# Building the gather table of a deformable convolution: four projected copies in PSUM, or one copy stored four times

## Chip, core and metric

The kernel runs on one NeuronCore of a Trainium2 chip. The metric is the device time of one execution in microseconds (us); of the kernel before, three executions were timed, and one more was profiled.

## The reference

Eight images of 56 x 56 pixels with 128 channels pass through four layers. Layer 1 is a selective-scan layer (called VSS here, a state-space scan in four directions). Layers 0, 2 and 3 are deformable convolutions, and the change is in these:

```python
xp = x @ w_in + b_in                                     # project every pixel
h = gelu(depthwise 3x3 conv of x, batch norm)
offset = (h @ w_off + b_off).reshape(N, H, W, 4, 9, 2)   # 4 groups, 9 points
mask = softmax((h @ w_msk + b_msk).reshape(N, H, W, 4, 9))
pad = jnp.pad(xp, 1)                                     # 58 x 58 padded pixels
# for each pixel, group and point: four corners, weighted bilinearly
samp = v(y0, x0)*w00 + v(y0, x0+1)*w01 + v(y0+1, x0)*w10 + v(y0+1, x0+1)*w11
y = einsum(samp, mask) @ w_out + b_out
x = x + gamma1 * layer_norm(y)
x = x + gamma2 * layer_norm(gelu(x @ w_fc1 + b_fc1) @ w_fc2 + b_fc2)
```

A group has 32 of the 128 channels. A corner's value is thus 32 floats, 128 bytes.

## The kernel before

**Stages.** One deformable layer on one image is a stage; there are 24, numbered 0 to 23 in the order of `stage_order`: (0,0), (0,1), ... with (layer, image) pairs of layers 0, 2 and 3 mixed. The scans of layer 1 run beside the stages, on the same engines.

**The table.** Each stage gathers from a table in DRAM (`table0` or `table1`, by the stage's parity). Row 4f + g of it belongs to padded pixel f and group g, and holds the four corners' 32 channels side by side, 512 bytes, so that one gathered row brings all four corners. The table of stage k+1 is made while stage k gathers.

**Making it.** A table step is `("at", k, i, 0)` on TensorE and `("at", k, i, 1)` on ScalarE and SyncE, i = 0 to 25, one for 128 padded pixels. TensorE projects the same pixels four times, shifted by 0, 1, 58 and 59 pixels (L1080), each with a one-row matmul that adds the bias and masks the border (L1081), into the four quarters of PSUM bank `d_pr1`. ScalarE copies the bank to `d_pst` (L834), with the channels put in the table's order, and SyncE stores 128 x 2048 bytes with one DMA (L573). `d_pst` is a single buffer: the copy of a step waits for the landing of the step before (semaphores `tab0` and `tab1`).

**Other ahead work.** The same bank `d_pr1` serves in turn the transposed input chunks (`ax`, L1068, loaded by `axl`, L548), the depthwise convolution (`ac`, L1092, stored by L580) and the offsets and masks of four pixel tiles (`pr`, L1104 on TensorE, then VectorE up to the indices `d_idx`, L1439). SyncE issues all these DMAs on one hardware queue, in the order of the program.

**Gathering.** GpSimd issues 882 indirect DMAs a stage (L674), 12 for each of the stage's 74 weigh steps, into one of five `d_g` buffers. VectorE weighs a buffer (L1247), TensorE adds it up (L943), and frees it. GpSimd starts a group of tiles only when its `d_idx` is there. The output chain of a pair of tiles (`ch`) follows.

**Order.** A planner (`Planner`) writes one list of items that every engine walks through in order. It puts scan steps and ahead steps between weigh steps. A scan step of a quiet kind takes a whole tick; the work behind a scan (`g`, `m`, `p`: gate, output projection, MLP, and the next image's projection) takes half ticks, and is thus packed twice as densely. I call that stretch the after-scan stretch: it lies in stages 3, 6, 8, 11, 13, 16, 18 and at the end of stage 20. `("ax", k, c)` for a layer-2 stage needs chunk c of the scan's output, which is stored by L651 and read back by L548 after a wait for the store's landing. Where a stage's work ahead is not done when its predecessor ends, the planner drains it there, while GpSimd has nothing to gather.

## Time and profile before

| | us |
|---|---|
| median of 3 runs (32655.79 to 32672.39) | 32657.38 |
| profiled execution, its own time | 32686.79 |
| span of the profiled execution | 32684.8 |
| GpSimd busy | 24416.8 (75%) |
| TensorE matmul busy | 24822.2 (76%) |
| VectorE busy | 22462.3 (69%) |
| ScalarE busy | 12136.3 (37%) |
| mean granted TensorE clock | 0.833 |

The span is the time from the first to the last instruction of the one core. Busy shares are of that span. The granted clock is 1 at 2.4 GHz and 0.5 at 1.2 GHz. GpSimd's time between two gathers is not counted as busy: the profile calls it issue.

### The profile page before, as it was taken

To read this page: it belongs to the slowest core of one execution; us is meant where nothing else is said; L and a number is where in the kernel's file an instruction comes from. 1 tells how busy PE (TensorE), PEld (TensorE's weight loads), DVE (VectorE), ACT (ScalarE), POOL (GpSimd) and SP (SyncE) were. 2 spreads that over 40 slices of the span, in tenths; PEclk is the share of its full clock that TensorE was granted. 3 is DMA by queue.
4 is the path that set the end of the run, shared out by engine and by line. 5 is a ranking of instruction groups with operands and counts; after the bars stand their busy time and mean duration, and the time that the engine had idled before them with its cause. 6 is when DMAs were issued, how large, how long until landed. Compare 5 with 4: busy or idle time off the path is not lost.

```text
span 32684.8 us, 293367 instructions
## 1 busy us (share of the span) xinstructions
PE 24822.2 (76%) x101616; PEld 16206.4 (50%) x101616; DVE 22462.3 (69%) x31704; ACT 12136.3 (37%) x20755; POOL 24416.8 (75%) x21172
## 2 busy tenths in 40 slices
PE   7587788877878788787877888778787887774544
PEld 5454455544545455455444555445444554454443
DVE  1278877888588868885888678876888688841211
ACT  1144434443444434443444444434444444420100
POOL 5777777777677777776777777777777777757767
PEclk6688888888888888888888888888888888886666
DMA  2211122111211121122111211112111221122211
GB/s 64 66 55 52 54 61 58 57 52 54 69 48 58 52 64 55 50 58 67 50 54 51 67 54 56 54 55 65 49 56 52 64 58 49 53 59 60 63 54 52
DMA packets 1191499, 1854.81 MB, mean 57 GB/s; under 512 B 388074, under 2 KB 747036, under 8 KB 1190012
## 3 DMA queue, kind: packets, MB, share of 16 engines
q0 software_dynamic: 677376, 1388.62, 15.2%
q1 hardware_dynamic: 512636, 447.43, 4.3%
q8 instruction: 803, 13.16, 0.2%
q14 instruction: 684, 5.60, 0.1%
HBM read 1569.35 MB, written 265.21 MB: 56 GB/s over the span
## 4 chain that ended last, share of the span: by engine, by line
POOL 64%; issue 18%; PE 13%; DVE 4%; ACT 1%; DMA 1%; SPq 0%; DVEq 0%; POOLq 0%; ACTq 0%
POOL d_g L674 64%; PE d_p L943 3%; DVE l_wk L1212 1%; PE d_pr L1081 1%; PE d_pr L1080 1%; PE d_pr L1092 1%; PE l_acc L929 1%; PE l_pm L978 1%; PE l_pc L1056 1%; DVE l_wk L1234 1%; DVE d_g L1247 1%; PE d_pr L1146 0%; DVE l_wk L1202 0%; PE l_pm L1031 0%; PE l_pm L1017 0%
## 5 line engine op out<-in xcount | busy, mean ns | idle before, releaser
L674 POOL DMA_INDIRECT d_g<-table,d_idx x21168 | 24416.6, 1153 | 8226.0 <-issue 6426.2
L943 PE MATMUL d_p<-d_g,c_ident 128*128 128x128 f32 x43200 | 6992.9, 335 | 3787.9 <-DVE d_g L1247 3786.3
L943 PEld LDWEIGHTS d_p<-d_g,c_ident 128*128 128x128 f32 x43200 | 6720.0, 247 | 4581.6 <-DVE d_g L1247 3658.1
L929 PE MATMUL l_acc<-l_wk,c_ident 128*128 128x448 f32 x14336 | 7141.1, 627 | 0.0
L1212 DVE TENSOR_TENSOR_SCAN l_wk<-l_wk,l_carry 128x448 f32<-128x448 f32 x6144 | 6715.0, 1133 | 0.0
L1247 DVE TENSOR_TENSOR d_g<-d_g,d_wt 128x1536 f32<-128x1536 f32 x1776 | 3103.7, 1748 | 5238.2 <-DMA d_g<-table,d_idx 5235.1
L1202 DVE TENSOR_TENSOR l_wk<-l_wk,l_pb 128x896 f32<-128x896 f32 x3584 | 3865.1, 1078 | 1585.0 <-PE l_pb L899 1577.0
L707 ACT ACTIVATE l_carry<-l_wk 128x2 f32<-128x2 f32 x3584 | 735.1, 205 | 10325.8 <-DVE l_wk L1212 10322.2
L717 ACT ACTIVATE l_wk<-l_wk,l_a 128x448 f32<-128x448 f32 x7168 | 4362.6, 656 | 14.2 <-DVE l_wk L1276 0.4
L929 PEld LDWEIGHTS l_acc<-l_wk,c_ident 128*128 128x128 f32 x14336 | 3100.6, 217 | 1820.9 <-issue 1699.3
L899 PE MATMUL l_pc<-l_spl,c_sel 96*128 96x448 bf16 x3584 | 1398.0, 390 | 3354.8 <-DVE l_wk L1234 3345.2
L1234 DVE TENSOR_TENSOR l_wk<-l_wk,l_pc 128x896 f32<-128x896 f32 x3584 | 3797.9, 1060 | 3.1 <-PE l_pc L899 2.4
L899 PEld LDWEIGHTS l_pc<-l_spl,c_sel 96*128 96x128 bf16 x3584 | 359.3, 100 | 4414.6 <-DVE l_wk L1234 4363.6
L899 PE MATMUL l_pb<-l_spl,c_sel 96*128 96x448 bf16 x3584 | 1355.9, 378 | 166.8 <-DVE l_wk L1202 158.5
L717 ACT ACT_TABLE_LOAD x1147 | 1471.6, 1283 | 20.0
L1081 PE MATMUL d_pr<-c_mix 1*128 1x128 f32 (+1 forms) x4992 | 1355.2, 355 | 0.0
L1080 PE MATMUL d_pr<-d_win,d_xt 128*128 128x128 f32 (+1 forms) x4992 | 1312.5, 349 | 37.0 <-ACT d_pst L834 23.3
L1092 PE MATMUL d_pr<-d_xt,d_diag 128*128 128x448 f32 x3024 | 1261.9, 557 | 7.6 <-ACT d_xt L825 5.2
L1080 PEld LDWEIGHTS d_pr<-d_win,d_xt 128*128 128x128 f32 (+1 forms) x4992 | 867.8, 211 | 496.1 <-issue 238.3
L1485 DVE BATCH_NORM_STATS2 d_bs<-d_pr 128x6 f32<-128x128 f32 (+1 forms) x1200 | 295.2, 285 | 1132.8 <-PE d_pr L1148 784.1
L1212 DVE TENSOR_TENSOR_SCAN l_wk<-l_wk 128x448 f32<-128x448 f32 x1024 | 1057.2, 1072 | 0.0
L1081 PEld LDWEIGHTS d_pr<-c_mix 1*128 1x128 f32 (+1 forms) x4992 | 824.8, 206 | 352.5 <-issue 106.6
(173 smaller groups left out, 22413.6 us busy)
## 6 DMA issues: line engine op xcount, KB each, us to landing
d_g<-table,d_idx POOLq DMA_INDIRECT x21168, 2.6
table<-d_pst SPq DMA_DIRECT2D x600, 256.0 KB
hd<-d_hst SPq DMA_DIRECT2D x168, 224.0 KB
d_htc<-hd SPq DMA_DIRECT2D x144, 256.0 KB
d_xin<-mid SPq DMA_DIRECT2D x112, 224.0 KB, 3.0
mid<-d_xo SPq DMA_DIRECT2D x192, 128.0 KB
d_xres<-mid SPq DMA_DIRECT2D x192, 128.0 KB
d_xin<-in_x SPq DMA_DIRECT2D x56, 224.0 KB, 3.1
```

The source lines that it names most:

```text
L674: e.indirect_dma_start(out=m.g[Q % SLOTS][:, j, :], out_offset=None, in_=m.table[k % 2], in_offset=bass.IndirectOffsetOnAxis(ap=m.idx[G % ...
L717: ins = e.activation(m.dA[(NSTEP * i + q) % 3][:, h, :], m.dt[P % 2][:, h, :], ACT.Exp, scale=m.aa[:, kd, h, n:n + 1])
L899: return e.matmul(bank[:, 0:448], m.sel[:, row + n:row + n + 1].to_broadcast([96, 128]), m.spl[P % 2][:, :], start=True, stop=True)
L929: ins = e.matmul(m.acc[:, h, 0:448], m.ident[:, :], m.hb[x % 4][:, h, :], start=(n == 0), stop=(n == 15))
L943: ins = e.matmul(m.p0[:, t % 2 * 128:t % 2 * 128 + 32 * w], m.ident[:, :], m.g[Q % SLOTS][:, w * p:w * p + w, 32 * r:32 * r + 32], start=( ...
L1080: e.matmul(m.r[1][0:n, cr * 128:cr * 128 + 128], m.xf[:, pos:pos + n], m.win[:, :], start=True, stop=False)
L1081: ins = e.matmul(m.r[1][0:n, cr * 128:cr * 128 + 128], m.mask[0:1, mo:mo + n], m.rowa, start=False, stop=True)
L1092: ins = e.matmul(m.r[1][:, 0:448], m.diag[:, j, :], m.xt[:, 8 * c + dy:8 * c + dy + 8, dx:dx + 56], start=(j == 0), stop=(j == 8))
L1202: e.tensor_tensor(m.hb[x % 4][:, :, :], m.dtu[P % 2][:, :, :], bc(m.pb[:, 0:448], 1, 2), ALU.mult).then_inc(s["f_pb"], 1)
L1212: ins = e.tensor_tensor_scan(m.hb[S % 4][:, h, way], m.dA[S % 3][:, h, way], m.hb[S % 4][:, h, way], ini, ALU.mult, ALU.add)
L1234: e.tensor_tensor(m.hb[x % 4][:, :, :], m.hb[x % 4][:, :, :], bc(m.pc[:, 0:448], 1, 2), ALU.mult).then_inc(s["f_pc"], 1)
L1247: e.tensor_tensor(g, g, wt, ALU.mult).then_inc(s["weighed"], 1)
```

## The change

Each padded pixel is projected once. The 3364 padded pixels are 27 tiles of 128; a table step now takes four tiles (`QUADS`, seven steps, the last with three tiles), one tile to each quarter of the bank. ScalarE copies the bank as it is. SyncE then stores each tile once for each corner: source row p, 128 floats, goes to the four group rows of padded pixel 128i + p - shift, at the corner's 128 bytes of each. That is 106 DMAs a stage with runs of 128 bytes, in place of 26 with runs of 2048 bytes. Most have 128 source rows; near the table's ends some have 127, 70, 69, 105, 106, 35 or 36.

```diff
+QUADS = [list(range(q, min(q + 4, 27))) for q in range(0, 27, 4)]
...
-        tables = deque((i, min(6, max(0, (128 * i + 127 + 59) // PW - 1) // 8)) for i in range(26))
+        tables = deque((j, min(6, max(0, (128 * x[-1] + 127) // PW - 1) // 8)) for j, x in enumerate(QUADS))
...
-        self.pst = sb("d_pst", [128, 4, 4, 32])
+        self.pst = sb("d_pst", [128, 4, 128])
...
+def corner(i, cr):
+
+    f0 = 128 * i - PW * (cr // 2) - cr % 2
+    p = max(0, -f0)
+    return f0 + p, p, min(128 * i + 128, PW * PW, NTAB + 128 * i - f0) - 128 * i - p
...   SyncE
-            e.dma_start(m.table[k % 2][f0 * 4:(f0 + n) * 4, :].rearrange("(p g) c -> p (g c)", g=4),
-                        m.pst[0:n].rearrange("p g r c -> p (g r c)")).then_inc(s[f"tab{T % 2}"], 16)
+            table = m.table[k % 2].rearrange("(f g) (r c) -> f g r c", g=4, c=32)
+            for x, i in enumerate(QUADS[j]):
+                for cr in range(4):
+                    first, p, n = corner(i, cr)
+                    if n > 0:
+                        e.dma_start(table[first:first + n, :, cr, :], m.pst[p:p + n, x, :].rearrange("p (g c) -> p g c", g=4),
+                                    ).then_inc(s[f"tab{T % 2}"], 16)
...   GpSimd, ahead of a stage's first gather
-        for b, v_ in enumerate(both(26 * k + 25)):
-            e.wait_ge(s[f"tab{b}"], v_)
+        for T in (7 * k + 5, 7 * k + 6):
+            e.wait_ge(s[f"tab{T % 2}"], J.tables(T))
...   ScalarE
-                e.wait_ge(s[f"tab{(T - 1) % 2}"], 16 * ((T - 1) // 2 + 1))
-            e.activation(m.pst[0:n], m.r[1][0:n, :].rearrange("p (r g c) -> p g r c", r=4, g=4),
-                         ACT.Copy).then_inc(s["f_r1"], 1)
+                e.wait_ge(s[f"tab{(T - 1) % 2}"], J.tables(T - 1))
+            whole = 4 if j < 6 else 2
+            ins = e.activation(m.pst[:, 0:whole, :], m.r[1][:, 0:128 * whole].rearrange("p (t c) -> p t c", c=128), ACT.Copy)
+            if j == 6:
+                ins = e.activation(m.pst[0:36, 2, :], m.r[1][0:36, 256:384], ACT.Copy)
+            ins.then_inc(s["f_r1"], 1)
...   TensorE
-            for cr in range(4):
-                pos = f0 + PW * (cr // 2) + cr % 2
+            for x, i in enumerate(QUADS[j]):
+                pos = 128 * i
+                n = min(128, PW * PW - pos)
...
-                e.matmul(m.r[1][0:n, cr * 128:cr * 128 + 128], m.xf[:, pos:pos + n], m.win[:, :], start=True, stop=False)
+                e.matmul(m.r[1][0:n, x * 128:x * 128 + 128], m.xf[:, pos:pos + n], m.win[:, :], start=True, stop=False)
```

The planner has 19 table steps fewer to place in each stage, so its list changes around them. Two places matter to the prediction. The first is SyncE's order of DMAs in stage 6, while it prepares stage 7, a layer-2 stage, beside the after-scan work: `mid<-l_xb` stores a chunk of the scan's output, `d_xin<-mid` reads it back for the table's stage, `l_wk<-xn`, `l_xb<-mid` and `l_wk<-mid` are loads of the after-scan work. Before:

```order
L573 DMA table<-d_pst 128x512
L651 DMA mid<-l_xb 112x4x128
L548 DMA d_xin<-mid 112x4x128
L643 DMA l_wk<-xn 128x448
L646 DMA l_xb<-mid 112x4x128
L626 DMA l_wk<-mid 112x4x128
L611 DMA d_xres<-in_x 128x2x128
L573 DMA table<-d_pst 128x512 x2
L633 DMA xn<-l_wk 128x448
```

The same place in the changed kernel:

```order
L589 DMA table<-d_pst 512x1x32
L589 DMA table<-d_pst 508x1x32
L589 DMA table<-d_pst 280x1x32
L589 DMA table<-d_pst 276x1x32
L589 DMA table<-d_pst 512x1x32 x12
L667 DMA mid<-l_xb 112x4x128
L561 DMA d_xin<-mid 112x4x128
L659 DMA l_wk<-xn 128x448
L662 DMA l_xb<-mid 112x4x128
L642 DMA l_wk<-mid 112x4x128
```

One DMA ahead of the chunk's store has become sixteen, with 512 runs each; the later single stores between the loads are gone.

The second place is TensorE at the end of stage 22, whose successor, stage 23, works on the same image. The first row adds up stage 22's last but one weigh step, the 128x64 rows with x12 its last one, and L1133 and L1139 are the output chain. Before, with the table steps shortened to their first pair:

```order
L943 MATMUL d_p<-d_g,c_ident 128x64 x24
L1080 MATMUL d_pr<-d_win,d_xt 128x128
L1081 MATMUL d_pr<-c_mix 128x128
...
L1133 MATMUL d_pr<-c_ident,d_x 128x128 x2
L1080 MATMUL d_pr<-d_win,d_xt 128x128
L1081 MATMUL d_pr<-c_mix 128x128
...
L943 MATMUL d_p<-d_g,c_ident 128x64 x12
L1139 MATMUL d_pr<-d_yt,d_fc 128x256 x4
```

The same place in the changed kernel:

```order
L961 MATMUL d_p<-d_g,c_ident 128x64 x24
L1150 MATMUL d_pr<-c_ident,d_x 128x128 x2
L961 MATMUL d_p<-d_g,c_ident 128x64 x12
L1156 MATMUL d_pr<-d_yt,d_fc 128x256 x4
L1163 MATMUL d_pr<-d_fc,d_ht 128x128 x4
```

Two table steps of eight matmul groups each stood ahead of the stage's last weigh step, and none does now.

## Rows read from the trace of the kernel before

**Rows 1.** The page: busy time of each engine, and the chain that ended last
```profile
PE 24822.2 (76%) x101616; PEld 16206.4 (50%) x101616; DVE 22462.3 (69%) x31704; ACT 12136.3 (37%) x20755; POOL 24416.8 (75%) x21172
...
POOL 64%; issue 18%; PE 13%; DVE 4%; ACT 1%; DMA 1%; SPq 0%; DVEq 0%; POOLq 0%; ACTq 0%
```

**Rows 2.** Waits of GpSimd: cause, us in total, times, longest
```profile
POOL d_g L674 <- issue: 6426.2, 21086, 0.3
POOL d_g L674 <- DVE d_idx L1439: 1384.2, 22, 270.0
POOL d_g L674 <- PE d_p L943: 415.2, 59, 30.5
```

**Rows 3.** Gathers alone, stages 21 and 12: window, length, busy (count), clock, DMA
```profile
29600.00:30235.00 635.00, 477.21 (x482) 0.66 0.20 56
17300.00:17860.00 560.00, 444.40 (x370) 0.85 0.18 52
```

**Rows 4.** Waits of GpSimd for TensorE within stages 3, 8, 13
```profile
POOL d_g L674 <- PE d_p L943: 28.1, 7, 12.2
POOL d_g L674 <- PE d_p L943: 47.1, 5, 22.7
POOL d_g L674 <- PE d_p L943: 34.0, 5, 14.8
```

**Rows 5.** Waits of GpSimd for indices after stages 1, 20, 22
```profile
POOL d_g L674 <- DVE d_idx L1439: 45.1, 1, 45.1
POOL d_g L674 <- DVE d_idx L1439: 221.5, 1, 221.5
POOL d_g L674 <- DVE d_idx L1439: 121.7, 1, 121.7
```

**Rows 6.** Timeline at the start: start, us, instruction, idle before
```profile
31.93 0.60 ACT L834 ACTIVATE d_pst<-d_pr 128x512 f32<-128x512 f32 x1 [5.95 <-PE d_pr L1081]
32.59 0.80 PE L1080 MATMUL d_pr<-d_win,d_xt 128*128 128x128 f32 x2 [0.69 <-ACT d_pst L834]
38.48 0.60 ACT L834 ACTIVATE d_pst<-d_pr 128x512 f32<-128x512 f32 x1 [5.95 <-PE d_pr L1081]
```

**Rows 7.** L1080, then L1081, up to 270 us: PE and PEld busy, clock, DMA
```profile
0.00:270.00 270.00, 76.39 (x208) 47.66 (x208) 0.69 0.16 51
0.00:270.00 270.00, 76.65 (x208) 47.75 (x208) 0.69 0.16 51
```

**Rows 8.** DMA queues in 40.2 to 43.3 us, around one input load
```profile
DMA packets 557, 0.39 MB, mean 125 GB/s; under 512 B 32, under 2 KB 480, under 8 KB 557
...
q1 hardware_dynamic: 557, 0.39, 38.8%
```

**Rows 9.** SyncE's table stores (ns of one issue), and landing of L548
```profile
L573 SPq DMA_DIRECT2D table<-d_pst x624: 319/320/975, 26.0 to 31492.0; - x156
...
DMA to landing us min/median/max: 2.6/3.1/6.9
```

**Rows 10.** Timeline between stages 22 and 23
```profile
31389.66 0.74 PE L1080 MATMUL d_pr<-d_win,d_xt 128*128 128x128 f32 x2
...
31401.94 5.38 PE L943 MATMUL d_p<-d_g,c_ident 128*128 128x64 f32 x24
...
31461.49 0.72 ACT L844 ACTIVATE d_hst<-d_pr,d_bnv 128x448 f32<-128x448 f32 x1 [7.12 <-PE d_pr L1092]
...
31492.41 0.33 SPq L603 DMA_DIRECT2D d_htc<-hd  x1
```

**Rows 11.** After-scan stretch of stage 6: all engines, then L1080 alone
```profile
8219.00:8620.00 401.00, 346.84 (x1602) 245.35 (x1602) 144.19 (x414) 150.73 (x213) 272.87 (x262) 0.86 0.29 83
8219.00:8620.00 401.00, 32.07 (x128) 21.24 (x128) 0.86 0.29 83
```

**Rows 12.** Idle before L1068 in all, and before L1292 in 8219 to 8640 us
```profile
DMA d_xin<-mid: 148.5, 34
...
DVE l_st L1292 <- DMA l_wk<-mid: 34.6, 5, 8.7
```

More of the change, by code:

```diff
@@ L485, in __init__, with tables @@
         self.total = total
+    def tables(self, T):
+        return sum(16 for x in range(T % 2, T + 1, 2) for i in QUADS[x % 7] for cr in range(4) if corner(i, cr)[2] > 0)
     def full(self, *key):
@@ L565, in sync_program @@
         elif kind == "at" and item[3] == 1:
-            _, k, i, _ = item
-            T = 26 * k + i
-            f0 = 128 * i
-            n = min(128, NTAB - f0)
-            if k >= 2 and i == 0:
-                e.wait_ge(s["weighed"], NQ * (k - 1))
-            e.wait_ge(s["f_r1"], J.free("t", k, i))
-            e.dma_start(m.table[k % 2][f0 * 4:(f0 + n) * 4, :].rearrange("(p g) c -> p (g c)", g=4),
-                        m.pst[0:n].rearrange("p g r c -> p (g r c)")).then_inc(s[f"tab{T % 2}"], 16)
+            _, k, j, _ = item
+            T = 7 * k + j
+            if k >= 2 and j == 0:
+                e.wait_ge(s["weighed"], NQ * (k - 1))
+            e.wait_ge(s["f_r1"], J.free("t", k, j))
+            table = m.table[k % 2].rearrange("(f g) (r c) -> f g r c", g=4, c=32)
[5 more added lines that the diff above has]
+                                    ).then_inc(s[f"tab{T % 2}"], 16)
         elif kind == "ac" and item[3] == 3:
@@ L827, in scalar_program @@
         elif kind == "at" and item[3] == 1:
-            _, k, i, _ = item
-            T = 26 * k + i
-            n = min(128, NTAB - 128 * i)
-            e.wait_ge(s["p_r1"], J.full("t", k, i))
+            _, k, j, _ = item
+            T = 7 * k + j
+            e.wait_ge(s["p_r1"], J.full("t", k, j))
             if T:
-                e.wait_ge(s[f"tab{(T - 1) % 2}"], 16 * ((T - 1) // 2 + 1))
-            e.activation(m.pst[0:n], m.r[1][0:n, :].rearrange("p (r g c) -> p g r c", r=4, g=4),
-                         ACT.Copy).then_inc(s["f_r1"], 1)
+                e.wait_ge(s[f"tab{(T - 1) % 2}"], J.tables(T - 1))
[4 more added lines that the diff above has]
+            ins.then_inc(s["f_r1"], 1)
         elif kind == "ac" and item[3] == 3:
@@ L1070, in tensor_program @@
         elif kind == "at" and item[3] == 0:
-            _, k, i, _ = item
-            f0 = 128 * i
-            n = min(128, NTAB - f0)
-            if i == 0:
+            _, k, j, _ = item
+            if j == 0:
                 e.wait_ge(s["da"], 48 * (k + 1))
-            e.wait_ge(s["f_r1"], J.use["t", k, i])
-            for cr in range(4):
-                pos = f0 + PW * (cr // 2) + cr % 2
+            e.wait_ge(s["f_r1"], J.use["t", k, j])
+            for x, i in enumerate(QUADS[j]):
+                pos = 128 * i
+                n = min(128, PW * PW - pos)
                 mo = pos if pos < PW else pos - 57 * PW + 290 if pos + n > 57 * PW else PW + pos % PW
-                e.matmul(m.r[1][0:n, cr * 128:cr * 128 + 128], m.xf[:, pos:pos + n], m.win[:, :], start=True, stop=False)
-                ins = e.matmul(m.r[1][0:n, cr * 128:cr * 128 + 128], m.mask[0:1, mo:mo + n], m.rowa, start=False,
+                e.matmul(m.r[1][0:n, x * 128:x * 128 + 128], m.xf[:, pos:pos + n], m.win[:, :], start=True, stop=False)
+                ins = e.matmul(m.r[1][0:n, x * 128:x * 128 + 128], m.mask[0:1, mo:mo + n], m.rowa, start=False,
                                stop=True)
```

## The prediction

> **What bounds the kernel now.** I read the page first. GpSimd is busy 75% of the span, and its issue time adds 6426.2 us, so 30,843 of 32,684.8 us are gathers; the chain that ended last says the same with POOL 64% and issue 18% [rows 1, 2]. Next come GpSimd's waits. There are only two kinds: 1384.2 us for indices, in 22 waits, of which 270.0 us is the start of the kernel, and 415.2 us for TensorE to free a `d_g` buffer [rows 2]. The change touches no gather, so all it can win is in these 1800 us, and it can lose by making new ones. TensorE at 76% and ScalarE at 37% are no bound by their shares.
>
> A gather's own time is the next thing to settle, since the change puts more packets in the hardware queue. In stage 21, where no scan runs, a gather takes 477.21 / 482 = 0.99 us; in stage 12, with the scan, 444.40 / 370 = 1.20 us, at a slightly lower DMA share [rows 3]. So it is the scan's work that stretches gathers, and DMA traffic doesn't follow it. I cost the extra traffic at nothing for GpSimd's own time; if it did cost, each 1% would be 244 us.
>
> The waits by place: most boundaries between stages cost 16 to 50 us (after stage 1, 45.1), but the one after stage 20 costs 221.5 and the one after stage 22 121.7 [rows 5]. By the planner's list, table steps still run in these two and at the start, and nowhere else: elsewhere they end 18 or more weigh steps before the stage's end, so those boundaries stay. The waits for TensorE lie in the after-scan stretches: 28.1, 47.1 and 34.0 us in stages 3, 8 and 13, 109 together [rows 4], and of the 415.2 the other 306 nearly all in stages 6, 11 and 16.
>
> **What a table step costs now.** At the start one follows the other every 38.48 - 31.93 = 6.55 us: eight groups of matmuls in 38.48 - 32.59 = 5.9 us, the last one's end included, so 0.725 us each, and 0.7 us for the copy and the turn [rows 6]. In 270 us the 26 steps hold TensorE for 76.39 + 76.65 = 153 us; neighbours overlap (0.80 us long, 0.725 us apart), so it is about 141 us of its time [rows 7]. The granted clock there is 0.69 in the mean, a mix of both levels. In stage 6 it is 0.86, and 128 records, 16 steps, take 32.07 us on L1080 [rows 11]; doubled for L1081, 4 us a step.
>
> **Removed.** Of 104 pairs of matmul groups a stage 27 stay. 26 copies become 7, with one small extra copy.
>
> Start: 141 x 77/104 = 104 us, and 19 turns of 0.7 us = 13 us: 117 us.
>
> Stages 3, 8, 13: the planner had 12 to 15 table steps, two or three depthwise chunks and input chunks at the after-scan stretch. Now it has placed all of that before the 33rd weigh step, ahead of the stretch. That is over 50 us of TensorE less (12 steps of 4 us), more than each wait of 28 to 47 us. I take all 109 us as gone. Gathers that then run beside VectorE's work, in place of waiting beside it, take about (1.20 - 0.99) / 1.20 = 18% longer, so 109 x 0.82 = 90 us are won.
>
> Stages 6, 11, 16: by the end of the stretch some 19 steps of 4 us (76 us) have gone, and 27 pairs (27 us) come in: close to 45 us less a stage, 135 us in all.
>
> After stage 22: two table steps stand ahead of the last weigh step and hold it from 31389.66 to 31401.94 us, 12.3 us, with the output chain behind it [rows 10]. They are gone. After the last depthwise copy at 31461.49 came five steps and then the offset load at 31492.41, 31 us [rows 10]; now two steps come, whose price follows.
>
> **Added: the bursts.** Each step now issues 16 DMAs (the last 10). An issue takes 0.32 us, some 0.37 us apart: 16 take 5.9 us [rows 9]. They hold 8192 runs of 128 bytes, 512 for each of 16 engines. No row of the kernel before shows a DRAM write in such short runs. From below: only the issue counts, 5.9 us a burst. From above: around one input load, 557 packets, most of them 512-byte rows, take 38.8% of 16 engines in 3.1 us, 34.6 ns each [rows 8]; 512 of those are 17.7 us. I take 12 us, in the middle, as a quarter of the bytes should make a packet shorter, not longer. The landing adds 2.6 us [rows 9]. Per stage that is 77 us of queue time spread over 1,350 us.
>
> The Trainium skill (DMA: Bandwidth & Descriptors, Specifications) puts the least transfer for full rate at 512 bytes and says that below it the engine reads, modifies and writes. It speaks against this change; no run here shows it yet, and I make it a rival below. The same page (Why a DMA increments its semaphore by 16 and not by 1) says that a DMA runs on the largest number of engines up to 16 that divides both sides' outer sizes; by it the 127-row store of the first step would use one engine, 508 runs. No row here shows that.
>
> Where do bursts cost? At the start they mostly lie beside 18 us of other TensorE work. The last two steps don't: ScalarE's copy of step 6 waits until the burst of step 5 has landed, 12 + 2.6 us, of which TensorE covers 4.4 us, and then ten issues (3.7 us) and some 3 us of data stand ahead of the offset load. About 17 us; start: 117 - 17 = 100 us won (between 9 and 25 for the tail: 92 to 108).
>
> After stage 22: 5.1 + 14.6 + 0.6 + 3.7 + 3 = 27 us in place of 31, plus the 12: 15 us won. After stage 20 three steps fewer, at 6.55 us or a bit more each, less the same tail: 15 us won.
>
> In stages 6, 11, 16 a burst goes out just before the chunk's store and read-back, and SyncE waits for the store's landing before it issues the read and all loads behind it (the order rows of SyncE). TensorE (L1068) and VectorE (L1292) wait for these loads, both in order, so weigh steps behind them are late. Already now TensorE waits 148.5 us in 34 times there, 4.4 us each, and VectorE up to 8.7 us [rows 12]. I count 11 bursts so placed in the three stages, 12 us each, 132 us; and some 12 more input chunks whose transposes follow their load directly, 4.4 us each, 53 us. With the 135 us off, these stages lose about 50 us, of which TensorE's idle 14% there (346.84 of 401 us busy [rows 11]) takes some: I put a loss of 35 us (from 55 won at 5.9 us a burst to 120 lost at 17.7).
>
> Elsewhere bursts lie 35 us or more apart beside the scan, and five `d_g` buffers of 17.5 us each (12 gathers of 1.20 + 0.30 us) cover a wait of 12 us. Without that cover it would be some 130 bursts at about 10 us each, 1,300 us.
>
> **Sum.** 100 + 15 + 15 + 90 - 35 = 185 us won. Against the profiled execution: span 32,685 - 185 = 32,500 us; its own time, 32,686.8, lies 2 us above the span. The median of runs lies 29 us below that, 32,657.4 - 185 = 32,472, rounded to 32,470 us.
>
> **Rivals.** (a) Gain eaten: bursts at the upper price of 17.7 us and nothing absorbed. Start 92, boundaries 5 each, stages 3, 8, 13 only 60, the three dense stages 120 lost: 40 us won, 32,620 us. For it: SyncE sits in front of every load. Against it: a packet with a quarter of the bytes.
>
> (b) Slower: a short DRAM write costs twice a 512-byte packet, 69 ns, 35 us a burst, from which the dense stages lose 11 x 35 + 53 - 135 = 300 us, the start is paced by bursts of 38 us (7 of them, 20 us lost), the two boundaries lose 15 each, and 90 are won: 260 us slower, 32,920 us. It turns at about 23 us a burst, 44 ns a write. For it: nothing here writes DRAM in runs under 512 bytes. Against it: even in the stretch around the input load [rows 8], with its mean of 700 bytes a packet, the price is only 34.6 ns, and I know no reason in these rows for twice that. The Trainium skill's rule of read-modify-write would be this case.
>
> (c) More won: all waits for TensorE go (415 x 0.82 = 340 us) with cheap bursts, and 110 + 25 + 25 us: 500 us, 32,160 us. Against it: the read-back chain in the dense stages stays.
>
> (d) No effect at all, since GpSimd sets the time: within 65 us, as in (a) with the start's gain lost too. Against it: the start's 117 us are TensorE's alone.
>
> **How the numbers follow.** The forecast, 100 to 330 us won, gets 0.6; (a) and (d) together 0.18; (b) 0.15; (c) 0.07. The forecast's own range is 32,330 to 32,590 us. 8 in 10: from 32,320 to 32,690 us, which leaves out (c), most of (b). A measurement of this kernel tells about 0.2%, 65 us, from no change. Faster by more: 0.6 + 0.07 + a small part of (a) = 0.68. Within it: 0.16. Slower: 0.16.
>
> **What would show it.** The first gather should start near 170 us. Stages 3, 8 and 13 should show no wait for TensorE. In stages 6, 11 and 16 waits of L1086 (the former L1068) and L1309 for DMA should be over 300 us, and GpSimd's waits for TensorE about as before. Landing of input loads, 3.1 us now, should have a tail to 15 us. Gathers should still take 0.99 us in stage 21. The prediction is wrong if a burst takes over 23 us, if gathers take longer beside bursts, or if ScalarE's wait for `tab` holds up the scan.

## The result, and the profile after

The changed kernel takes 32290.69 us (median of 4 runs, 32266.03 to 32311.03) against 32656.58 us of the kernel before (4 runs beside it, 32650.71 to 32672.39): ratio 0.9887, 95% interval 0.987 to 0.9904, 366 us less. I had forecast 185 us less and a range down to 32,320 us: the right direction, half the size, and just outside the range.

The head of the page after the change, the waits of GpSimd in the whole span (us, times, longest), and the chain that ended last:

```profile
span 32297.3 us, 279615 instructions
...
PE 23220.6 (72%) x94224; PEld 14960.8 (46%) x94224; DVE 22461.6 (70%) x31704; ACT 11892.0 (37%) x20322; POOL 24335.8 (75%) x21172
...
q1 hardware_dynamic: 1731788, 447.55, 6.2%
...
POOL 71%; issue 19%; PE 6%; DVE 2%; ACT 1%; DMA 1%; SPq 1%; POOLq 0%; DVEq 0%; ACTq 0%
```
```profile
POOL d_g L690 <- issue: 6434.7, 21115, 0.3
POOL d_g L690 <- DVE d_idx L1456: 1291.3, 24, 197.6
POOL d_g L690 <- PE d_p L961: 193.4, 29, 18.8
```

TensorE gave up 4 points of its share and stays off the bound; in the chain that ended last it has 6% where it had 13%. Of GpSimd's two kinds of wait, that for TensorE more than halved (from 415.2) and that for indices fell by 93 (from 1384.2) [rows 2]; GpSimd's own busy time fell by 81 us as well [rows 1], which nothing in my working foresaw. Two waits between stages (after stages 10 and 15, 30.5 and 25.6 us) are put down to TensorE before and to indices after. Like with like, TensorE's fell from 359 to 193 us and the indices' from 1440 to 1291.

The span is 387.5 us shorter. To place it I took, for each of the 24 stages, the time from its first gather to the end of its last, and the gap to the next stage, out of both traces:

```
place                                before     after   difference
first gather begins                   282.1     166.8     -115.3
stages 3, 8, 13                      3969.3    3873.5      -95.8
stage 18                             1297.1    1281.0      -16.1
stages 6, 11, 16                     4112.8    4059.7      -53.1
gap after stage 20                    221.2     197.3      -23.9
gap after stage 22                    121.4     104.3      -17.1
the other 17 stages                 21822.9   21749.4      -73.5
the other gaps                        820.6     827.6       +7.0
```

(The first line counts from some 11.6 us before the page's zero.) The first wait and the waits after stages 20 and 22, as GpSimd shows them, answer to 270.0 [rows 2] and to [rows 5]:

```profile
POOL d_g L690 <- DVE d_idx L1456: 155.2, 1, 155.2
...
POOL d_g L690 <- DVE d_idx L1456: 197.6, 1, 197.6
...
POOL d_g L690 <- DVE d_idx L1456: 104.6, 1, 104.6
```

Stage by stage, stage 3 shows no wait for TensorE any more, and stages 8 and 13 show what is left of [rows 4]:

```profile
POOL d_g L690 <- PE d_p L961: 2.8, 1, 2.8
...
POOL d_g L690 <- PE d_p L961: 0.3, 1, 0.3
```

**The end of the start.** The timeline from 116 to 147 us shows the tail that the last two table steps leave:

```profile
121.02 0.60 ACT L850 ACTIVATE d_pst<-d_pr 128x512 f32<-128x512 f32 x1 [3.49 <-PE d_pr L1098]
121.64 21.33 SPq L589 DMA_DIRECT2D table<-d_pst  x26
...
134.04 0.38 ACT L850 ACTIVATE d_pst<-d_pr 128x256 f32<-128x256 f32 x1 [12.42 <-DMA table<-d_pst]
...
143.02 0.52 SPq L619 DMA_DIRECT2D d_htc<-hd  x1
```

ScalarE's copy of step 6 waits 12.42 us for the stores of step 5, and then ten more issues stand in SyncE's queue ahead of the offset load. From the copy of step 5 to the offset load it is 143.02 - 121.02 = 22.0 us.

**The burst.** One issue of a table store, and the landing of an input load (DMA from issue to landing, us); then the DMA queue over 11 us in which a burst runs nearly alone (packets, MB, share of 16 engines):

```profile
L589 SPq DMA_DIRECT2D table<-d_pst x2544: 512/639/5614, 25.9 to 31105.5; - x196
```
```profile
DMA to landing us min/median/max: 2.5/3.1/5.8
```
```profile
q1 hardware_dynamic: 7541, 0.94, 55.0%
```

An issue takes 0.64 us and not 0.32 as before [rows 9]: 16 of them 10.2 us. The packets take 0.55 x 16 x 11 / 7541 = 12.8 ns each, so 512 for an engine are 6.6 us. A burst is paced by SyncE's issues and not by its data. No input load took more than 5.8 us to land, so where a load is late it is because SyncE hasn't issued it.

The first burst of each stage is longer, 15.5 to 17.0 us, where the others take 10.9 us at the median. Its third store takes some 5 us to issue, and it stands behind the store with 127 source rows, 508 runs. Here is that third store in stage 0's table, and the hardware queue in 28 to 32 us, while SyncE is held up:

```profile
L589 SPq DMA_DIRECT2D table<-d_pst x1: 5028/5028/5028, 27.3 to 27.3; - x1
```
```profile
q1 hardware_dynamic: 375, 0.05, 9.5%
```

In these 4 us 375 packets start, one every 10.7 ns, where the burst above starts 7541 in 11 us, one every 1.5 ns. In e4, where the same 127 rows are 127 runs, no issue takes over 2.1 us.

**The dense stretch.** After-scan stretch of stage 6, the same 401 us of the stage as in [rows 11]: all engines, then L1097 (the former L1080) alone; then what ended TensorE's idle time before L1086 in it, and GpSimd's waits for TensorE in it (49.3 us in 7 times before the change):

```profile
8061.00:8462.00 401.00, 316.72 (x1461) 219.28 (x1462) 144.75 (x415) 149.71 (x209) 257.10 (x248) 0.86 0.34 86
...
8061.00:8462.00 401.00, 11.09 (x48) 7.63 (x48) 0.86 0.34 86
```
```profile
PE d_pr L1086 <- DMA d_xin<-mid: 42.1, 6, 8.7
```
```profile
POOL d_g L690 <- PE d_p L961: 69.2, 7, 12.2
```

TensorE does 42 us less on the two table lines (2 x 32.07 before, 2 x 11.09 now) and waits 42 us for input chunks. SyncE's timeline shows what stands in front of two of these loads:

```profile
8126.48 15.72 SPq L589 DMA_DIRECT2D table<-d_pst  x16
8142.24 0.63 SPq L667 DMA_DIRECT2D mid<-l_xb  x1
8145.11 0.31 SPq L561 DMA_DIRECT2D d_xin<-mid  x1
...
8236.46 10.87 SPq L589 DMA_DIRECT2D table<-d_pst  x16
8247.38 0.62 SPq L667 DMA_DIRECT2D mid<-l_xb  x1
...
8250.25 0.32 SPq L561 DMA_DIRECT2D d_xin<-mid  x1
```

That is the order I had forecast, burst in front of chunk store in front of read-back, and bursts of about the length that I had forecast (10.9 to 15.7 us). In stage 6 the trade came out at a loss of 5 us. But stages 11 and 16 won 17 and 41 us. Over the whole span the waits for input loads are, by L1086's own row and by TensorE's two queues apart (us, times):

```profile
DMA d_xin<-mid: 349.0, 65
```
```profile
PEld d_pr L1086 <- DMA d_xin<-mid: 178.5, 33, 10.3
PE d_pr L1086 <- DMA d_xin<-mid: 170.4, 32, 10.0
...
DVE l_st L1309 <- DMA l_wk<-mid: 266.5, 45, 18.6
```

The row by line adds up the weight load's wait and the matmul's, which are the same wait. I had read its 148.5 us in 34 times [rows 12] as 34 waits of TensorE; they are 17, of 72.4 us, and they lie in the whole span and not in the three dense stages, where my prediction put them. TensorE waits 98 us more than before. In the three dense stages it is 116.8 us in 18 waits against 20.8 in 4; stage 6 has the 42.1 us above.

### The profile page after: what moved, and what is told of

It is laid out like the page before. It is cut to its first block, busy times and chain, and to the rows that moved or that the text cites. A ratio compares the mean times of both kernels' runs of the same rounds, so it can differ in the third digit from the quotient of the medians.

```text
span 32297.3 us, 279615 instructions
## 1 busy us (share of the span) xinstructions
PE 23220.6 (72%) x94224; PEld 14960.8 (46%) x94224; DVE 22461.6 (70%) x31704; ACT 11892.0 (37%) x20322; POOL 24335.8 (75%) x21172
## 4 chain that ended last, share of the span: by engine, by line
POOL 71%; issue 19%; PE 6%; DVE 2%; ACT 1%; DMA 1%; SPq 1%; POOLq 0%; DVEq 0%; ACTq 0%
POOL d_g L690 71%; PE d_p L961 2%; PE d_pr L1109 1%; SPq L589 1%; DVE l_wk L1229 0%; PE l_pc L1074 0%; PE l_pm L996 0%; DVE d_g L1264 0%; PE d_pr L1163 0%; DMA d_g<-table,d_idx 0%; PE l_acc L947 0%; PE d_pr L1123 0%; DMA mid<-l_xb 0%; PE l_pm L1049 0%; PE l_pm L1035 0%
## 5 line engine op out<-in xcount | busy, mean ns | idle before, releaser
L1219 DVE TENSOR_TENSOR l_wk<-l_wk,l_pb 128x896 f32<-128x896 f32 x3584 | 3866.5, 1079 | 989.3 <-PE l_pb L917 982.7
L1109 PEld LDWEIGHTS d_pr<-d_xt,d_diag 128*128 128x128 f32 x3024 | 588.5, 200 | 586.9 <-issue 559.4
L996 PE MATMUL l_pm<-l_yx,l_diag 128*128 128x448 f32 x2016 | 822.4, 546 | 4.1 <-ACT l_xb L775 4.1
L1156 PE MATMUL d_pr<-d_yt,d_fc 128*128 128x256 f32 (+1 forms) x2496 | 738.0, 424 | 93.2 <-ACT d_ht L902 72.5
L917 PEld LDWEIGHTS l_pb<-l_spl,c_sel 96*128 96x128 bf16 x3584 | 371.2, 104 | 933.2 <-DVE l_wk L1219 589.6
```

The source lines that it names most:

```text
L917: return e.matmul(bank[:, 0:448], m.sel[:, row + n:row + n + 1].to_broadcast([96, 128]), m.spl[P % 2][:, :], start=True, stop=True)
L996: ins = e.matmul(m.pm[:, 0:448], m.cdiag[:, 9 * h + j, :], m.grid[:, h, 8 * c + dy:8 * c + dy + 8, dx:dx + 56], start=(j == 0), stop=(j == 8))
L1109: ins = e.matmul(m.r[1][:, 0:448], m.diag[:, j, :], m.xt[:, 8 * c + dy:8 * c + dy + 8, dx:dx + 56], start=(j == 0), stop=(j == 8))
L1156: ins = e.matmul(bank[:, f * 256:f * 256 + nt * n], m.fc1[:, (2 * f2 + f) * 128:(2 * f2 + f) * 128 + 128], m.x1t[:, 0:nt * n], start=True, ...
L1219: e.tensor_tensor(m.hb[x % 4][:, :, :], m.dtu[P % 2][:, :, :], bc(m.pb[:, 0:448], 1, 2), ALU.mult).then_inc(s["f_pb"], 1)
```

## The experiments

They ran in three groups, each on a chip of its own, with the kernel before timed beside each: 32742.42 us, 35339.29 us and 35890.94 us. On the second and third chip the changed kernel's engines wait for up to 107 us at a time with no cause that the profile names ("remote", "issue"), and GpSimd waits for TensorE ten times as long as on the first, nearly half of it in stages where the first shows no such wait; there I use ratios and differences between kernels of one group alone. In the first group (runs 1 to 4) the changed kernel wasn't run; its trace and that of the kernel before are those of the result above. A gather that nothing disturbs takes 944 ns in both and in e2, but 947 ns in e1, e3 and e4 (and in e5), so the times of these are some 64 us too long beside them (3 ns on each of 21,168 gathers), 8 us of it in the dense stages; the ratios, with the kernel before timed beside, don't show it. Stage 21, before the change and in e3:

```profile
L674 POOL DMA_INDIRECT d_g<-table,d_idx x482: 940/944/2520, 29599.8 to 30222.8; - x161
```
```profile
L690 POOL DMA_INDIRECT d_g<-table,d_idx x450: 943/947/2531, 29399.6 to 29998.6; - x150
```

"Dense" below is the sum of stages 6, 11 and 16, read as in the table above. Each such number is from one trace. What each run was to show stands as it was written before it ran.

**1. e2_short_in_before.** The kernel before with the new form of store: four copies of its 512 results, each as runs of 128 bytes.

```diff
-            e.dma_start(m.table[k % 2][f0 * 4:(f0 + n) * 4, :]..., m.pst[0:n]...)
+            for cr in range(4):
+                e.dma_start(table[f0:f0 + n, :, cr, :], m.pst[0:n, cr, :].rearrange("p (g c) -> p g c", g=4))
```

> The kernel before, with its four-fold projection and 26 table steps, but each step's bank is copied plainly and stored by four DMAs with runs of 128 bytes in place of one with runs of 2048. It holds the price of short runs alone. If short runs cost nothing that matters (13 ns a packet in the trace of the changed kernel): 32,640 to 32,680 us. If short runs or the issues in front of other loads cost, as my forecast for the dense stages had it: 30 to 150 us slower than before. If the plain copy or the short stores make gathers shorter: GpSimd busy falls from 24,417 us toward 24,336 and the time by up to 80 us.

Measured: 32754.81 us, ratio 1.0004 (0.9995 to 1.0013); dense 4118.1 us against 4112.8.

```profile
L575 SPq DMA_DIRECT2D table<-d_pst x2496: 512/639/1952, 25.4 to 31505.7; - x192
```

Four times the issues, each twice as long, and sixteen times the packets (128 bytes in place of 2048) cost nothing that can be measured, as long as the issues come four at a time. That ends my rival (b): a short write is not dear. These stores all have 128 or 105 source rows, none has 127.

**2. e1_fourfold.** The changed kernel, with each matmul pair of a table step issued four times. TensorE then has the work of before and a little more (108 pairs a stage, not 104), in 7 lumps of 18 to 23 us a stage and not in 26 of 3.3 to 5.9 us.

```diff
+                for _ in range(4):
                     e.matmul(m.r[1][0:n, x * 128:x * 128 + 128], m.xf[:, pos:pos + n], m.win[:, :], ...)
                     ins = e.matmul(m.r[1][0:n, x * 128:x * 128 + 128], m.mask[0:1, mo:mo + n], ...)
```

> The changed kernel, but each pair of projection matmuls of a tile is issued four times, so TensorE has the table work of before (108 pairs of groups a stage), while planner, copies and stores are those of the changed kernel. Theory A (the gain is TensorE time at the start, at two boundaries and in the after-scan stretches): nearly all of the 366 us is lost again, 32,560 to 32,650 us, with the first gather near 265 us and GpSimd's waits for TensorE back over 350 us. Theory B (the gain behind the start comes from fewer table steps and copies, and from their new places): only the start and the two boundaries are lost, some 140 us, so 32,430 us, and GpSimd's waits for TensorE stay near 193 us.

Measured: 33587.51 us, ratio 1.0254 (1.024 to 1.0268), far above what either theory gave. GpSimd waits:

```profile
POOL d_g L690 <- DVE d_idx L1457: 1490.0, 24, 261.0
POOL d_g L690 <- PE d_p L961: 915.7, 108, 38.9
```

The start is back (261.0 us), and dense is 4397.2 us, 337 more than after the change. Both theories had left out the size of a lump, four times that of before. Two more things differ from the kernel before and aren't separated here: the stores go out in bursts of 16, and the granted clock is 0.812 in the mean where it was 0.833, with TensorE busy for 25656.0 us where it was 24822.2.

**3. e3_singles.** The changed kernel with one tile a step: 27 steps a stage, four stores a step.

```diff
-QUADS = [list(range(q, min(q + 4, 27))) for q in range(0, 27, 4)]
+QUADS = [[q] for q in range(27)]
...
```

> The changed kernel with one tile a table step (27 steps of one pair of matmul groups, one small copy and four stores), so that the planner's order is nearly that of before, with TensorE's table work cut to a quarter. Theory A: the after-scan stretches gain as in the changed kernel (waits for TensorE under 200 us), while the start gains less, since each copy waits for the stores of the step before (27 steps of about 5.5 us): first gather near 250 us, total 32,350 to 32,420 us. Theory B (the order of the seven large steps does it): waits for TensorE stay over 300 us and the total is 32,550 to 32,640 us.

Measured: 32413.56 us, ratio 0.9898 (0.9883 to 0.9913). Dense is 3996.3 us: 116.5 less than before and 63 less than after the change. What it wins there it gives back at the start, where the first gather comes 64 us later, since ScalarE's copy waits for the landing of the step before (the second row is of the first 320 us):

```profile
POOL d_g L690 <- DVE d_idx L1454: 219.6, 1, 219.6
...
ACT d_pst L850 <- DMA table<-d_pst: 96.7, 21, 9.8
```

Theory A has it: GpSimd waits 148.7 us for TensorE in all. The run also bounds my terms for the dense stages. With the TensorE work gone and the steps as small as before, they win 116.5 us; the four-tile steps take 63 us of it back. That 63 is for all that comes with four tiles: bursts of 16 issues, lumps of four tiles on TensorE, and another order. TensorE's waits for input loads in these stages are 11.9 us in 2 waits in e3, and 116.8 in 18 after the change.

Stages 3, 8 and 13 take 3902.4 us, 67 less than before, and GpSimd still waits 43 us for TensorE in them, where the changed kernel has 3. So there the work that is gone gives some two thirds of the 96 us, and the rest comes with fewer steps that end ahead of the stretch.

**4. e4_long_runs.** The changed kernel, its copies stored in whole rows of 512 bytes, which leaves the table with the wrong layout: same 16 issues, a quarter of the packets.

```diff
-            table = m.table[k % 2].rearrange("(f g) (r c) -> f g r c", g=4, c=32)
+            table = m.table[k % 2].rearrange("(f r) c -> f r c", r=4)
...
-                        e.dma_start(table[first:first + n, :, cr, :], m.pst[p:p + n, x, :].rearrange("p (g c) -> p g c", g=4),
+                        e.dma_start(table[first:first + n, cr, :], m.pst[p:p + n, x, :],
```

> The changed kernel with the same number of stores and bytes, but each source row goes out as one run of 512 bytes (the corners' channels of all groups side by side, so the table's rows hold the wrong channels and the output is not the reference's). 55,000 short packets a stage become 14,000. If the length of runs matters in the dense stages: 30 to 100 us faster than the changed kernel. If only the 106 issues count: the same within 20 us.

Measured: 32301.53 us, ratio 0.9864 (0.9849 to 0.9879), 0.2% under the changed kernel's own ratio, with intervals that overlap. Dense 4045.2 us (14 less), the start 8.7 us less. TensorE waits 95.0 us for input loads in the dense stages, in 18 waits as after the change. An issue takes 0.43 us in place of 0.64; the burst is 7 us in place of 10. Whether the 30 to 100 us or the "same within 20 us" of the expectation came can't be told: the ratios say 75 us, the dense stages 14.

```profile
L589 SPq DMA_DIRECT2D table<-d_pst x2544: 257/432/2122, 25.4 to 31114.8; - x196
```

**5. a2_changed_again, and 6. e5_pairs.** The changed kernel as the reference of the second group; and two tiles a step with two halves of `d_pst` used in turn, so that a copy waits for the stores of the step before last.

```diff
-QUADS = [list(range(q, min(q + 4, 27))) for q in range(0, 27, 4)]
+QUADS = [list(range(q, min(q + 2, 27))) for q in range(0, 27, 2)]
...
-            if T:
-                e.wait_ge(s[f"tab{(T - 1) % 2}"], J.tables(T - 1))
+            if T >= 2:
+                e.wait_ge(s[f"tab{T % 2}"], J.tables(T - 2))
...
```

> The changed kernel once more, on the same chip as the three kernels beside it, to compare them directly and to see how much its gathers' busy time (24,336 us, 81 us less than before in the first profile) varies from one profile to the next. If the shorter gathers are the change's: busy again within 15 us of 24,336. If they are chance: anywhere from 24,330 to 24,450.

> Table steps of two tiles (14 a stage), with two halves of the store buffer used in turn, so that a copy waits only for the stores of the step but one before. Theory A' (the gain is TensorE time, and large lumps of table work and stores cost in stages 6, 11 and 16): start like the changed kernel's (first gather 155 to 175 us), dense stages like those of single-tile steps (their waits for TensorE under 110 us in all, changed kernel 182), total 50 to 80 us faster than the changed kernel. Rival (lumps don't matter, only the start does): the same as the changed kernel within 20 us.

Measured: 34974.18 us, ratio 0.9901 (0.9877 to 0.9925), and 34925.0 us, 0.9876 (0.9848 to 0.9904). Dense 4443.8 and 4413.7 us, the start the same (166.5 and 165.9). The change keeps its ratio on this chip. Pairs can't be told from steps of four, and GpSimd waits 528.9 us for TensorE in the dense stages, where under 110 was expected. Yet TensorE's waits for input loads in the dense stages nearly went: 29.9 us in 6 waits, against 135.4 in 16 in the changed kernel beside it. That is 105 us of waits less, as much as from the changed kernel to e3, for 30 us of time. GpSimd's busy time in a2, 24511.7 us, fits neither of the two answers expected of it: no trace of the kernel before was taken on this chip, and it is 176 us above that of the same kernel in the first trace.

**7. e6_four_issues.** One store a tile, which sends each row of 512 bytes four times over (wrong layout again): 4 issues a step, not 16.

```diff
-                for cr in range(4):
+                    e.dma_start(table[128 * i:128 * i + n, :, :], bc(m.pst[0:n, x, :], 1, 4))
```

> The changed kernel with one store a tile, which writes the tile's rows four times side by side in runs of 512 bytes (the table holds the wrong channels, so the output isn't the reference's): 4 issues a step in place of 16, the same bytes and runs as e4_long_runs. If SyncE's issues ahead of the read-back (16 of 0.64 us, 11 us) are what makes L1086 wait in the dense stages: that wait falls from 349 us to under 220 us and the time by 30 to 80 us. If it is the order (input load directly ahead of its transposes): the wait stays over 280 us and the time within 20 us of the changed kernel.

Measured: 34796.95 us, ratio 0.9842 (0.9814 to 0.9869), 177 us under the changed kernel beside it (98 between the two profiled executions). Dense is 27 us less, the start 11, stages 0 to 23 without the dense and the after-scan ones 106. So 12 of 16 issues are worth some 0.5% on this chip, and not mainly in the places where I had looked for it: in those other stages GpSimd's waits for TensorE fell from 723 to 583 us, and on the first chip there are none of them.

Neither of the two answers expected of this run came. The row of the input load's waits was to fall from 349 us to under 220 if the issues ahead of the load make the waits, and to stay over 280 if the order of the steps does. It stands at 337.3 us, and at 381.5 in the changed kernel beside it; in the dense stages TensorE waits 113.6 us in 17 waits, against 135.4 in 16:

```profile
DMA d_xin<-mid: 337.3, 60
```

So most of these waits do not come from the length of the burst.

**8. e7_singles_fourfold.** One tile a step, each matmul pair four times: the work and the lumps of before, with the new stores.

```diff
-QUADS = [list(range(q, min(q + 4, 27))) for q in range(0, 27, 4)]
+QUADS = [[q] for q in range(27)]
...
+                for _ in range(4):
```

> Single-tile table steps (as e3_singles), each pair of projection matmuls issued four times: TensorE's table work of the kernel before in lumps of its size, with short stores. Theory A' (amount and lump size of TensorE's table work explain everything): like the kernel before, within 60 us, and thus some 850 us under e1_fourfold. Rival (short stores or single-tile order cost by themselves): over 100 us slower than before.

Measured: 35454.4 us, ratio 1.0023 (1.0007 to 1.004). With the matmuls back in small lumps, the whole gain is gone and hardly more (115 us, where under 60 was expected). Beside e1 (1.0254) this shows both halves: the gain is TensorE's work, and the same work in lumps four times as long costs another 2.3%. That is a comparison of two ratios from two chips, and it takes in the larger bursts of e1; by e3 and the changed kernel (0.9898 and 0.9887) the larger steps without the fourfold matmuls cost nothing in all.

**9. a3_changed_third, and 10. e8_singles_two_slots.** The changed kernel as the reference of the third group; and the single steps of e3, with two slots in turn (the edit is shown against e3).

```diff
-            if T:
-                e.wait_ge(s[f"tab{(T - 1) % 2}"], J.tables(T - 1))
-            ins = e.activation(m.pst[0:n, 0, :], m.r[1][0:n, 0:128], ACT.Copy)
+            if T >= 2:
+                e.wait_ge(s[f"tab{T % 2}"], J.tables(T - 2))
+            ins = e.activation(m.pst[0:n, T % 2, :], m.r[1][0:n, 0:128], ACT.Copy)
```

> The changed kernel once more, on the chip of the next two, as their reference. Against the kernel before 0.987 to 0.990, as in its first two comparisons.

> 27 table steps of one tile a stage, but ScalarE's copy of a step waits for the stores of the step before last instead of the last. Theory A (single steps are held only by the landing of their own stores; the size of a share costs nothing at this load): the first gather near 165 us instead of 219 us of the singles before, no waits of d_pst for table stores over 30 us in all, stage durations as in the singles before (6, 11, 16 near 1,330 us), ratio to the kernel before 0.986 to 0.988, so level with the four-tile steps or 50 us under them. Theory B (what singles save in TensorE's dense stages is lost in other places whatever the slots): ratio 0.989 to 0.991.

Measured: 35435.83 us, ratio 0.9876 (0.9842 to 0.991), and 35389.57 us, 0.9855 (0.9819 to 0.989). The waits for the stores at the start halved, from 96.7 to 49.3 us, and did not go, as four issues and a landing are longer than two steps:

```profile
ACT d_pst L850 <- DMA table<-d_pst: 49.3, 14, 9.0
```

The first gather comes 24 us after that of the changed kernel (188.5 against 164.1, where I had expected 165), and dense is 4399.2 against 4461.8: 63 us less, the same number as on the first chip. The sum, 46 us or 0.13%, is within what can be told from no change. This kernel has the lowest ratio of the versions with the right table, but I can't call it faster than the change. Four tiles a step at the start and single ones later wasn't tried.

**11. e9_stores_twice.** Each store issued twice, the second into a table that nobody reads: bursts of 32.

```diff
-                    if n > 0:
+                    for table in tables if n > 0 else []:
                         e.dma_start(table[first:first + n, :, cr, :], ...)
```

> The changed kernel, with each table store issued twice, the second time into a spare table that nobody reads: bursts of 32 issues of 0.64 us, 20 us each, twice the packets of 128 bytes. Theory A (the readback waits that a burst causes in the dense stages are covered by the ring of d_g buffers): waits of L1086 for DMA rise by some 200 us, GpSimd's waits for TensorE by less than 60 us, the tails at the start and after stages 20 and 22 grow by some 10 to 20 us each, ratio to the kernel before 0.989 to 0.992, 50 to 100 us over the changed kernel. Theory B (my forecast's term: a burst costs its own length at 11 places in the dense stages): 132 us more there and 100 us more elsewhere, ratio 0.994 to 0.998.

Measured: 35814.5 us, ratio 0.9985 (0.9963 to 1.0006): 379 us over the changed kernel beside it. The first gather comes 76 us later, the gaps after 20 and 22 grow by 32 us, dense by 125 us. Waits of TensorE for the input load, and of GpSimd for TensorE, in the changed kernel and then here:

```profile
PE d_pr L1086 <- DMA d_xin<-mid: 195.2, 31, 16.6
```
```profile
POOL d_g L690 <- PE d_p L961: 1926.9, 239, 33.2
```
```profile
PE d_pr L1087 <- DMA d_xin<-mid: 293.0, 31, 24.9
```
```profile
POOL d_g L691 <- PE d_p L962: 2361.0, 249, 34.7
```

TensorE's waits for loads rise by 98 us (by 195 as the row by line adds them, as expected), but GpSimd's for TensorE by 434, where theory A gave under 60: it falls. Theory B was low in all, but its part for the dense stages, 132 us, is near the 125 measured. There TensorE's waits for loads go from 143.3 to 244.9 us, and VectorE's for `l_wk<-mid`, which stand behind the same bursts, from 98.4 to 194.3; so the 125 us can't be put down to TensorE's waits alone. And 231 of the 434 us lie in the 17 other stages, where the first chip has no such wait at all.

## Why the prediction was off, step by step

**Start** (100 forecast, 115 measured). Right, and it is TensorE's work: with that work back the first gather is late again (261.0 us in e1, 265.5 in e7). The tail was forecast at about 17 us in its parts; the two parts seen, the copy's wait and the ten issues behind it, are 12.4 and 8.4 us.

**After stages 22 and 20** (15 and 15 forecast, 17 and 24 measured). Right, and the second somewhat low.

**Stages 3, 8, 13** (90 forecast, 96 measured). Right, and by the mechanism named: their waits went from 109 to 3 us, and gathers took 6 us longer in return, where the forecast had 19. By e3 some two thirds of this is the work that is gone and the rest the fewer steps. Stage 18, 16 us, I had left out; 13 of it are shorter gathers (below) and 4 a wait for TensorE that is gone.

**Dense stages 6, 11, 16** (35 lost forecast, 53 won measured). This is the step that failed, and in it the charge of 132 us for "11 bursts so placed, 12 us each". The sum was 135 for TensorE's work, less 132 for the bursts and 53 for "some 12 more input chunks", with some 15 us taken up by idle time. The runs, one trace each, with waits and lengths of the three stages in us:

```
run              issues    TensorE's waits    GpSimd's waits   length
                 a step    for input loads    for TensorE
before              1       20.8 in  4           244.6         4112.8
after              16      116.8 in 18           190.2         4059.7
e3_singles          4       11.9 in  2           104.8         3996.3
e4_long_runs       16       95.0 in 18           169.8         4045.2
second chip:
a2_changed_again   16      135.4 in 16           571.9         4443.8
e5_pairs            8       29.9 in  6           528.9         4413.7
e6_four_issues      4      113.6 in 17           533.8         4417.2
third chip:
a3_changed_third   16      143.3 in 18           553.7         4461.8
e8_singles          4       11.5 in  2           490.4         4399.3
e9_stores_twice    32      244.9 in 18           696.8         4587.3
```

TensorE's work gave 116.5 us in e3 for the 135 forecast. The count was about right: 14 waits more than before, and 11 of the 18 have a burst right in front of the chunk's store in SyncE's timeline. Their price is what was wrong. They are 96 us more where 185 were charged, and only part of them reached GpSimd. The 11 with a burst in front are 7.2 us long in the mean, the 7 without one 5.4 us, and the 4 before the change were 5.2. No burst makes these 5 us: the chunk's store takes 2.4 to 3 us to land and the read-back some 3 us more, and TensorE, whose next work in order is the transposes, waits for both. A burst adds little to that: with 4 issues in place of 16 (e6) 17 waits are left, 22 us shorter in all, and the time is 27 us less; with shorter issues (e4) all 18 are left, 22 us shorter, and it is 14 us less. With another order of the steps (e3, e5, e8) 2 or 6 waits are left. All that comes with four-tile steps, bursts included, cost 63 us in the dense stages (e3, and e8 on its own chip), where 185 had been charged to the loads alone.

Why the bursts cost so little here is argued and not shown: I had reckoned with five `d_g` buffers of cover elsewhere in the span, and left it out here because TensorE was 86% busy; the change itself took that down to 79% in stage 6 (316.72 of 401 us). That such cover has an end is seen in e9, where 16 issues more cost 125 us. No single rate turns these waits into time: 105 us of them less go with 63 us (e3) or 30 us (e5).

**The short writes** (rival (b), 0.15). Refuted by e2. The Trainium skill (DMA: Bandwidth & Descriptors, Specifications) says that transfers under 512 bytes are read, modified and written; the trace doesn't bear out that this is dear here: 12.9 ns a packet in the mean, against 28.2 ns for a packet of 512 bytes, and no time in e2. What the same page says of engines and outer sizes, by which I had put the 127-row store on one engine, the trace bears out. By it each engine that a DMA runs on writes the semaphore once (Why a DMA increments its semaphore by 16 and not by 1). Packets of 4 bytes, counted in the traces' hardware queue, are 65,582 after the change and 36,230 before. The difference, 29,352, is what the page's rule gives for the two kernels' stores; with 16 engines for every store it would be 30,720. SyncE loses 5 us by that store in each stage, as seen above; what this costs in time no run shows.

**Gathers' own time** (no change forecast, 81 us less measured). In stage 21 it is as forecast:

```profile
29229.00:29864.00 635.00, 477.78 (x485) 0.66 0.19 55
```

477.78 / 485 = 0.99 us, as in [rows 3]. Taken apart, a gather in which no VectorE work falls takes 944 to 945 ns in the mean in both traces (5876 and 5800 of them), so the queue's extra packets cost it nothing. The 81 us are in gathers during which a VectorE instruction begins: 1256 ns in the mean before (13592 of them), 1248 after (13707); with the product `l_wk<-l_wk,l_pb` of L1219, 1386 and 1368 ns. They make up the whole of the 73.5 us that the other 17 stages gave (their gathers' busy time is 73 us less) and 13 of stage 18's 16. Whose doing it is stays open. GpSimd's busy time, with the 64 us for the longer undisturbed gather taken off where it applies, is 24,336, 24,354 and 24,313 us in the three traces with a quarter of the table's matmuls (after, e3, e4), 24,417 and 24,452 us in the two with all of them in small steps (before, e2), and 24,660 us in e1, with all of them in large lumps. That points to TensorE's table work. But it is one trace each, on the second and third chip kernels with equal work lie up to 100 us apart, and no run shows by what way TensorE's work would reach a gather. So this is the part of the result, some 80 us, that I can't account for.

**Rivals (a) and (d)** are refuted by the size of the gain; **(c)**, 500 us by all waits for TensorE gone, is too: 193.4 us of them are left, 190.2 of these in the dense stages, as it was said there.

**What the profile was to show.** No wait in stages 3, 8 and 13, and gathers of 0.99 us: so. L1086 over 300 us: 349.0 by the row that I had named, which counts each wait twice; L1309 not, 266.5. GpSimd's waits for TensorE in the dense stages "about as before": they fell from 244.6 to 190.2 us, which is the whole gain there. A tail of landings to 15 us: none over 5.8, since the bursts delay the issue of a load and not its flight.

## What to carry to other kernels

When a wait is moved from one engine to another, it must be priced at the engine that sets the time, behind the idle time and the buffers in between, and with the load as it is after the change, not before; and then at twice its length too, since that cover may be spent by then. Before a wait is put down to the burst in front of it, ask how long it would be without the burst: here store, landing and read-back made most of it. A view that groups waits by line can count one wait on two queues of an engine. The size of a lump counts as much as the sum of the work: the same matmuls in lumps of 18 to 23 us, with stores to match, cost 2.3% over lumps a quarter as long. A store that is split into more issues should be priced by the issue time of its own form, on the queue that the loads share, before its bytes are; and a cut that leaves 127 rows in place of 128 should be looked at by itself.

## What the hardware showed that I had not expected

One issue by SyncE takes 0.32 us for 128 rows of 2048 bytes side by side, 0.43 us for 128 rows of 512 bytes apart, and 0.64 us for 512 runs, whether they are of 128 or (e6) of 512 bytes: it goes with how the store is cut up, not with its bytes. The issue behind a 127-row store took 5.0 us, while that store's packets started one at a time. A DRAM write of 128 bytes takes 12.9 ns of a DMA engine, less than half of that of 512 bytes. An undisturbed gather of GpSimd takes 944 ns in the mean beside 79,000 hardware-queue packets of the table's stores or beside 1.27 million, but 1365 to 1368 ns when a scan of VectorE begins inside it, and 944 again when it lies wholly inside one VectorE instruction.
